# A two-layer post-norm decoder: the last step of the second attention, and who writes the two parts of the experts' down weights

## The chip, the cores and the metric

The program runs on one core of a Trainium2 chip. The metric is the time of one execution in microseconds (us), and the figure given for a kernel is the median of its runs. A core has TensorE (matrix products and transposes, PE in the profile; PEld is its weight load), VectorE (DVE), ScalarE (ACT), GpSimd (POOL) and SyncE (SP, which here only starts transfers). Each engine works through its own list of instructions in order; semaphores order them against each other. Matrix products and transposes write PSUM, eight banks of 512 float32 words per partition; the other working memory is SBUF.

## The reference

x has shape (4, 256, 256): four batches of 256 rows. Six sublayers follow one another, each in the form x = layernorm(x + f(x)):

```
x = LN(x + attention0(x));  x = LN(x + quantised cross product(x, fside, ctx));  x = LN(x + ternary FFN(x))
x = LN(x + attention1(x))          # stage 3 below: 16 heads, window 64, 4 sinks, output projection Wo
x = LN(x + cross attention(x, ctx))# stage 4: x @ softmax(q k^T), one 256x256 product per batch
x = LN(x + experts(x))             # stage 5: 8 experts, top 2, inner size 176
# experts:
probs = softmax(x @ gate_w.T);  combine = the two largest, divided by their sum
g, u = split(x @ w1[e].T);  out += combine[e] * (silu(g) * u) @ w2[e].T
```

All arithmetic is float32.

## The kernel before, in words

**Numbering.** A sublayer is a stage: 3 is the second attention, 4 the cross attention, 5 the experts. P is 128, S and D 256, B 4 batches; a pair is two batches. `x` holds the rows; `transpose_x(stage, lo, hi)` (L1856) turns the rows of some batches on TensorE into PSUM, and ScalarE's `evac_xT` (recorded at L813, the line of its helper `copy`) copies them to `xT`, from which the products of that stage read.

**Two parts.** The experts' products run in a float32 format that keeps fewer bits of an operand (fp32r), so each operand is split into a high part, the value rounded by writing it to that format, and a low part, the value less the high part. The up weights (`mw1H`, `mw1L`), the down weights (`mw2H`, `mw2L`) and x (`xH`, `xL`) have both. `up(n)` (L2424) makes 12 matmuls for one of 22 tiles of 512 columns, `down(n)` (L2441) 12 more.

**Weight groups.** Weights are loaded by DMA and turned by TensorE in groups of up to four 128x128 transposes into one bank (`pe_groups`, L397); the list is `G`, and `PLAN` has for each group its bank, the engine that copies it out, that engine's count, and the group that used the bank last. Groups 19 to 30 (NGM to NG2) are the 12 of the up weights, of 4, 4, 3, 4, 4, 3, ... transposes, 44 in all, in banks 0 and 1 in turn. VectorE writes their high part by a copy and their low part by a subtraction from PSUM (`evac_parts`, L1468 and L1469). They are turned beside the second attention: `beside(L, step, g)` gives the groups of each quarter step. Groups 31 to 36 (NG2 on) are the six of the down weights, 4 transposes each and 2 in the last, in banks 3 and 2 in turn. ScalarE copies each twice, to the high part and in full to `mw2f` (memory of `PT`); GpSimd subtracts the one from the other (L792). GpSimd also writes x's low part of the first pair for the experts (L787, semaphore `x_low0`).

**The second attention** (`attn_back(1)`) has six steps, 0 to 5, of four quarters g, each for four heads. In step s the scores' maxima of batch s are found and the exponentials, values and outputs of batch s-2 made; steps 4 and 5 so have only the latter. A quarter of TensorE in steps 4 and 5 is: `exp_scores(n)`, `values(n-1)` (L2084, L2087), the weight groups of `beside`, in g=1 `transpose_outputs` of the batch before (L2118), in g=2 its `project_outputs` (L2125), and `output_rows(n-1)` (L2094). VectorE in a quarter: `evac_parts` of the groups, in g=2 `attention_residual` (L1196), `divide_outputs` (L1411, L1415), and `norm_stats(3, 0)` in g=2 of step 4, `norm_apply(3, 0)` in g=0 of step 5. ScalarE: three exponentials (L957) and copies.

**After the last quarter** TensorE has this order: `transpose_x(4, 0, 2)`, once all up groups are copied out; `values(15)`; `context(0)`, the cross attention's product of batch 0 (L1869); `output_rows(15)`; `context(1)`; `transpose_outputs(3)`; `project_outputs(3)`; the six down groups; `transpose_x(5, 0, 2)`; `up(0)`; `logits(0)` (L2392); `up(1)`; `transpose_x(4, 2, 4)`; `context(2)`; `combine(0)` (L2400), which turns the experts' weights that VectorE's `router(0)` (L1729 to L1750) has made; `context(3)`; and then the loop `up(n)`, `down(n-2)` for n from 2 to 21. `up(1)` waits until all down groups are copied out, since it writes their banks, and `up(2)` for VectorE's `gated(0)` (L1765), which reads what `combine(0)` gave.

VectorE: `context_residual(0)`, `divide_outputs(15)`, `context_residual(1)`, `norm_stats(4, 0)` and `norm_apply(4, 0)` (L1207, L1216, L1223; between the two GpSimd makes the inverse deviations, L693 and L694), `attention_residual(3)`, `norm_stats(3, 2)`, `norm_apply(3, 2)`, `router(0)`, `copy_combine(0)`, `gated(0)`.

Of the kernel before, what the change touches and what calls it, by code (L numbers as in the profile page):

```python
# [5 lines left out]
def post_ln_decoder_two_layers(nc: bass.Bass, t: dict, out: bass.AP):  # L6
# [37 lines left out]
    with ExitStack() as ctx:  # L44
# [178 lines left out]
        mw2f = words_of(PT_words, 0, [P, EC, D])  # L223
# [84 lines left out]
        x_low0 = sem("x_low_part_of_pair0")  # L308
        mw2_low = sem("mw2_low_part")
# [43 lines left out]
        for c0 in range(0, EC, 2):  # L353
            n = min(2, EC - c0)
            group([m2n[:, r, c::EC] for c in range(c0, c0 + n) for r in range(2)],
                  [m[:, c0:c0 + n, :].rearrange("p a b -> p (a b)") for m in (mw2H, mw2L, mw2f)], P, n * 256, False, "m2")
# [11 lines left out]
        for k in range(len(G)):  # L368
            bank_ = k % 2 if k in BESIDE else 2 + k % 2 if k >= NG2 else k % 4
            eng_ = "act" if k >= NG2 or k in SHARED else "dve" if k in BESIDE or k % 2 else "act"  # L370
# [29 lines left out]
        def evac_groups(eng, copy, lo, hi, name):  # L400
            for k in range(lo, hi):
                srcs, dst, rows, cols, half, need = G[k]
                if PLAN[k][1] == name:
                    eng.wait_ge(wt_done, k + 1)
                    src = (bank16 if half else bank)(PLAN[k][0], cols, 0, rows)
                    if need == "m2":

                        copy(dst[0], src)
                        dst = dst[2]
                    copy(dst, src).then_inc(wt_act if name == "act" else wt_dve, 1)  # L410
# [25 lines left out]
        def xT_bank(stage, b):  # L436
# [3 lines left out]
            return b if stage == 4 and b < 2 else 6 + b % 2  # L440
# [13 lines left out]
        def beside(L, step, g):  # L454
# [5 lines left out]
            return lo + (hi - lo) * slot // (LAG * NG), lo + (hi - lo) * (slot + 1) // (LAG * NG)  # L460
# [191 lines left out]
        def _(pool):  # L652
# [131 lines left out]
            for b in range(2):  # L784
                bs = slice(b * S, (b + 1) * S)
                pool.wait_ge(xT_ready, turned(5, b))
                alone(pool.tensor_tensor(xL[5][:, :, bs], xT[:, :, bs], xH[5][:, :, bs].bitcast(F32), ALU.subtract),  # L787
                      x_low0)
            for k in range(NG2, len(G)):
                pool.wait_ge(wt_act, PLAN[k][2])  # L790
                high, low, full = G[k][1]
                alone(pool.tensor_tensor(low, full, high.bitcast(F32), ALU.subtract), mw2_low)  # L792
# [10 lines left out]
        def _(act):  # L803
# [156 lines left out]
            def attn_back(L):  # L960
                a = A[L]
                for step in range(STEPS):
                    for g in range(NG):
# [15 lines left out]
                        if g == 1 and step > LAG:  # L979
                            copy_OT(L, step - LAG - 1)  # L980
                if L == 1:
                    evac_xT(4, 0, 2)
                copy_outputs(L, B * NG - 1)
# [150 lines left out]
            evac_groups(act, copy, NG2, len(G), "act")  # L1134
            evac_xT(5, 0, 2)

# [31 lines left out]
        def _(dve):  # L1168
# [292 lines left out]

            def evac_parts(lo, hi):
# [19 lines left out]
            def attn_back(L):  # L1482
# [34 lines left out]
                if L == 1:  # L1517
                    context_residual(0)
                if L == 0:

                    copied_out(dve, NGM)
                    weight_maxima(0)
# [1004 lines left out]
```

## Time and profile before

| what | us |
|---|---|
| median of 3 runs | 480.86 |
| the runs | 477.39, 480.86, 483.25 |
| the profiled execution | 483.25 |
| its span, first to last instruction | 481.2 |
| outside the span | 2.05 |
| granted TensorE clock over the span, share of full speed | 0.932 |

A profile is one execution, recorded by the hardware. The busy time of an engine is the time in which it had an instruction under way; what stands in square brackets after an instruction is the idle time of its engine before it, and what ended it. A matmul's end is modelled, so starts are the better marks. All times below are us from the start of the span.

### The profile page before, as it was taken

The page shows a single profiled execution, that of the slowest core. Times are in us where ns is not written, and L with a number is a line of the kernel's source. Part 1 is how long each engine was busy: PE and PEld are TensorE (multiplying, and loading weights), DVE is VectorE, ACT ScalarE, POOL GpSimd, SP SyncE. Part 2 cuts the span into 40 slices and gives each one's busy share as a digit, 9 for nine tenths or more (in the row PEclk, how much of TensorE's full clock was granted, in tenths as well). Part 3 has the DMA queues.
Part 4 walks back from the last instruction along what each step waited for, and adds up shares of the span by engine and source line. Part 5 has one row for each costly group of instructions (what it writes and reads, how often), then busy time and mean ns, then how long its engine had stood idle before and what let it go on. Part 6 is the DMA issues. An engine that isn't in the chain of part 4 may idle for free.

```text
span 481.2 us, 8198 instructions
## 1 busy us (share of the span) xinstructions
PE 415.0 (86%) x3126; PEld 316.6 (66%) x3128; DVE 330.6 (69%) x768; ACT 245.5 (51%) x458; POOL 113.9 (24%) x134
## 2 busy tenths in 40 slices
PE   3976877999787776999997889999986999999993
PEld 2534644677655555789565755667665789888883
DVE  2499897777779888556567695458734685756555
ACT  1296903656646967566588434555516333523221
POOL 5500005538622451151563000001005310001001
PEclk9989797999999666699999899999988999999998
DMA  6900020000000000000000049810000000000101
GB/s 192 306 33 1 2 74 3 2 3 3 2 1 1 0 2 0 1 0 2 1 1 1 1 61 111 147 55 1 0 1 0 1 1 1 1 0 2 44 1 44
DMA packets 13126, 13.33 MB, mean 28 GB/s; under 512 B 2904, under 2 KB 12448, under 8 KB 12832
## 3 DMA queue, kind: packets, MB, share of 16 engines
q1 hardware_dynamic: 12224, 12.54, 11.5%
q8 instruction: 25, 0.41, 0.3%
q10 hardware_dynamic: 864, 0.27, 0.2%
q14 instruction: 13, 0.11, 0.1%
HBM read 11.56 MB, written 1.05 MB: 26 GB/s over the span
## 4 chain that ended last, share of the span: by engine, by line
PE 64%; DVE 20%; ACT 8%; DMA 3%; issue 3%; POOL 1%; SPq 0%; ACTq 0%; DVEq 0%; POOLq 0%
PE PS L2424 12%; PE PS L2441 6%; PE PS L1979 4%; ACT arena L813 4%; PE PS L2348 4%; PE PS L2084 4%; DVE mx L1400 3%; PE PS L397 3%; PE PS L2125 3%; PE PS L2364 3%; PE PS L2001 3%; PE PS L2052 3%; DMA arena<-mT 2%; DVE mx L1395 2%; PE PS L2094 2%
## 5 line engine op out<-in xcount | busy, mean ns | idle before, releaser
L957 ACT ACTIVATE PT<-PS 128x512 f32<-128x512 f32 x96 | 53.5, 595 | 35.9 <-PE PS L2052 35.8
L2424 PE MATMUL PS<-arena_r 128*128 128x512 f32 x264 | 66.0, 399 | 2.2 <-ACT xT L813 2.2
L2424 PEld LDWEIGHTS PS<-arena_r 128*128 128x128 f32 x264 | 49.2, 193 | 12.2 <-issue 2.6
L693 POOL TENSOR_SCALAR va<-mv 128x4 f32<-128x4 f32 x11 | 5.2, 475 | 195.9 <-DVE mv L1216 195.9
L813 ACT ACTIVATE arena<-PS 96x1024 bf16<-96x1024 bf16 (+6 forms) x59 | 42.2, 767 | 15.7 <-PE PS L1979 6.1
L1395 DVE TENSOR_REDUCE mx<-PS 128x4 f32<-128x512 f32 x32 | 21.9, 685 | 22.9 <-PE PS L2020 22.9
L2001 PE MATMUL PS<-masks,ident 128*128 128x512 bf16 x80 | 30.8, 386 | 5.8 <-DVE mx L1400 2.7
L2441 PEld LDWEIGHTS PS<-arena_r 128*128 128x128 f32 x264 | 34.4, 191 | 1.8 <-DVE arena_r L1773 0.2
L1400 DVE TENSOR_REDUCE mx<-PS 128x4 f32<-128x1024 f32 (+1 forms) x32 | 35.0, 1092 | 0.6 <-PE PS L2035 0.6
L1979 PE MATMUL PS<-ident,arena 128*96 128x128 bf16 x416 | 28.1, 229 | 8.1 <-ACT arena L813 4.7
L2441 PE MATMUL PS<-arena_r 128*128 128x256 f32 x264 | 35.0, 283 | 0.0
L1765 DVE TENSOR_TENSOR V<-PS,xb 128x512 f32<-128x512 f32 x22 | 15.2, 689 | 27.9 <-PE PS L2424 27.7
L1979 PEld LDWEIGHTS PS<-ident,arena 128*96 128x96 bf16 x416 | 26.1, 130 | 12.0 <-POOL arena L765 4.2
L1155 ACT ACTIVATE V<-PS 128x512 f32<-128x512 f32 x22 | 13.2, 600 | 37.1 <-PE PS L2424 37.1
L712 POOL TENSOR_SCALAR_AFFINE_SELECT PT<-PT 128x512 f32<-128x512 f32 x16 | 11.9, 741 | 70.3 <-ACT PT L957 70.0
L813 ACT ACTIVATE arena_r<-V 128x512 fp32r<-128x512 f32 x22 | 13.9, 632 | 24.9 <-DVE V L1769 24.9
L2084 PE MATMUL PS<-PT,V 128*32 128x256 f32 x256 | 21.1, 401 | 4.4 <-ACT PT L957 3.9
L1294 DVE COPY arena<-PS 96x1024 bf16<-96x1024 bf16 x32 | 21.0, 680 | 5.5 <-PE PS L1979 5.4
L2052 PE MATMUL PS<-arena 99*128 99x256 bf16 x128 | 22.7, 280 | 0.5 <-DMA arena<-mT 0.5
L2032 PE MATMUL PS<-arena 96*128 96x256 bf16 (+1 forms) x128 | 22.6, 264 | 0.4 <-DVE mx L1400 0.4
L397 PE MATMUL PS<-ident,arena 128*128 128x128 f32 (+2 forms) x150 | 21.0, 279 | 1.6 <-ACT PT L813 1.6
L813 ACT ACTIVATE OS<-PS 128x256 f32<-128x256 f32 x32 | 12.3, 384 | 18.4 <-PE PS L2087 18.4
(247 smaller groups left out, 949.8 us busy)
## 6 DMA issues: line engine op xcount, KB each, us to landing
arena<-in_L_ffn_w SPq DMA_DIRECT2D x16, 176.0 KB, 10.4
arena<-in_L_ffn_w SPq DMA_DIRECT2D x2, 1024.0 KB, 10.3
arena<-in_L_ffn_w SPq DMA_DIRECT2D x2, 704.0 KB, 6.7
arena<-in_fside_BxS2xS SPq DMA_DIRECT2D x1, 1024.0 KB, 12.2
out<-x SPq DMA_DIRECT2D x4, 256.0 KB, 2.2
x<-in_x SPq DMA_DIRECT2D x1, 768.0 KB, 9.1
arena<-in_L_attn_Wq SPq DMA_DIRECT2D x2, 256.0 KB, 4.5
arena<-in_L_attn_Wo SPq DMA_DIRECT2D x2, 256.0 KB, 6.1
```

Source lines behind the costliest of these rows:

```text
L397: last = nc.tensor.transpose(o, s, (ident16 if half else ident)[0:K, 0:K])
L813: return nc.scalar.activation(dst, src, ACT.Copy)
L957: nc.scalar.activation(PT[:, n % 2, 512 * j:512 * (j + 1)], bank(3 + j), ACT.Exp, scale=NEG_SCALE)\
L1395: v.tensor_reduce(mx[:, b % 2, 0, HG * g:HG * g + HG], bank(set_).rearrange("p (h s) -> p h s", h=HG), X, ALU.max).then_inc(a["mx"], 1)
L1400: v.tensor_reduce(mx[:, b % 2, 1, HG * g:HG * g + HG], PS[:, set_ + 1:set_ + 3, :].rearrange("p a (h s) -> p (a h) s", h=2) [:, :, 0:late_ ...
L1979: last = nc.tensor.transpose(bank16(4 + n % 4, P, i * P, STK), s_, ident16[:, :])
L2001: mm(out_, ident16[:, :], mk[:, cols].unsqueeze(1).to_broadcast([P, n_heads, cols.stop - cols.start]), start=start, stop=not start)
L2032: mm(bank(bk, keys.stop - keys.start, i * S), Qh[0:STK, b, h, P:S], K_[0:STK, b, kv(h), keys], start=(i == 0), stop=False)
L2052: last = mm(bank(bk, S, i * S), K_[0:R, b, kv(h), 0:P], Qh[0:R, b, h, :], start=(causal and i == 0), stop=(i == 1))
L2084: mm(PS[VW * i:VW * (i + 1), ob, 0:S], V1[:, 2 * b, kv(HG * g + i), :], p0[:, i, :], start=True, stop=False)
L2424: last = mm(bank(2 * (n % 2) + gu), wp[c][:, gu, c_ * P:(c_ + 1) * P], xp[5][:, c, blk * 512:(blk + 1) * 512], start=(step == 0 and c == 0 ...
L2441: last = mm(bank(4 + 2 * blk + k // 2, D, (k % 2) * D), amP[:, n % 3, part, k * P:(k + 1) * P], wp[:, c_, :], start=(c_ == 0 and k % 2 == ...
```

## The change

- **Down weights.** ScalarE makes one copy of each down group, the high part, and raises `m2_high`; VectorE writes the low part from PSUM (`m2_low`) and frees the bank. `mw2f`, the second copy and GpSimd's six subtractions go. TensorE turns the six groups two at a time in three places.
- **x's low part** of the first pair for the experts is made by VectorE (`low_x(5, 0, 2)`) and no longer by GpSimd.
- **Up groups.** `beside` deals the 12 out to six quarters, two each, so that the last two quarters have none.
- **Stage 4's turn and products.** `transpose_x(4, 0, 2)` moves into quarter g=2 of the last step, `context(0)` and `context(1)` into g=3.
- **Banks.** `transpose_x(5, 0, 2)` writes banks 4 and 5 and not 6 and 7, once the last exponentials have read them.
- **Order.** On TensorE `logits(0)` goes ahead of `up(0)` and `combine(0)` ahead of `context(2)`. On VectorE both context residuals and `norm_stats(4, 0)` go ahead of `divide_outputs(15)`; the low parts, `norm_stats(3, 2)` and `low_x(5, 0, 2)` stand among the rest as the diff shows.

```diff
@@ PLAN, evac_groups
-            eng_ = "act" if k >= NG2 or k in SHARED else "dve" if k in BESIDE or k % 2 else "act"
+            eng_ = "act" if k in SHARED else "dve" if k >= NG2 else "dve" if k in BESIDE or k % 2 else "act"
...
-                        copy(dst[0], src)
-                        dst = dst[2]
-                    copy(dst, src).then_inc(wt_act if name == "act" else wt_dve, 1)
+                        copy(dst[0], src).then_inc(m2_high, 1)
+                    else:
+                        copy(dst, src).then_inc(wt_act if name == "act" else wt_dve, 1)
@@ xT_bank, beside
-            return b if stage == 4 and b < 2 else 6 + b % 2
+            if b < 2 and stage >= 4:
+                return b if stage == 4 else 4 + b
+            return 6 + b % 2
...
-            return lo + (hi - lo) * slot // (LAG * NG), lo + (hi - lo) * (slot + 1) // (LAG * NG)
+            slots = LAG * NG if L == 0 else LAG * NG - 2
+            return min(hi, lo + (hi - lo) * slot // slots), min(hi, lo + (hi - lo) * (slot + 1) // slots)
@@ gpsimd
-            for b in range(2):
-                bs = slice(b * S, (b + 1) * S)
-                pool.wait_ge(xT_ready, turned(5, b))
-                alone(pool.tensor_tensor(xL[5][:, :, bs], xT[:, :, bs], xH[5][:, :, bs].bitcast(F32), ALU.subtract),
-                      x_low0)
-            for k in range(NG2, len(G)):
-                pool.wait_ge(wt_act, PLAN[k][2])
-                high, low, full = G[k][1]
-                alone(pool.tensor_tensor(low, full, high.bitcast(F32), ALU.subtract), mw2_low)
@@ scalar, attn_back
+                        if L == 1 and step == STEPS - 1 and g == 2:
+                            evac_xT(4, 0, 2)
+                copy_outputs(L, B * NG - 1)
                 if L == 1:
-                    evac_xT(4, 0, 2)
-                copy_outputs(L, B * NG - 1)
+                    evac_groups(act, copy, NG2, NG2 + 2, "act")
                 copy_OT(L, B - 1)
@@ scalar, after attn_back(1)
-            evac_groups(act, copy, NG2, len(G), "act")
+            evac_groups(act, copy, NG2 + 2, NG2 + 4, "act")
             evac_xT(5, 0, 2)
+            evac_groups(act, copy, NG2 + 4, len(G), "act")
@@ vector
+            def m2_low(lo, hi):
+
+                for k in range(NG2 + lo, NG2 + hi):
+                    _, (high, low), rows, cols, _, _ = G[k]
+                    dve.wait_ge(m2_high, k - NG2 + 1)
+                    v.tensor_tensor(low, bank(PLAN[k][0], cols, 0, rows), high.bitcast(F32), ALU.subtract).then_inc(wt_dve, 1)
@@ vector, attn_back
                 if L == 1:
                     context_residual(0)
+                    context_residual(1)
...
+                if L == 1:
+                    norm_stats(4, 0)
                 divide_outputs(L, B * NG - 1)
                 if L == 1:
-
-                    context_residual(1)
-                    norm_pair(4, 0)
+                    m2_low(0, 2)
+                    norm_apply(4, 0)
...
                 attention_residual(L, B - 1)
+                if L == 1:
+                    m2_low(2, 4)
@@ vector, after attn_back(1)
-            norm_pair(3, 2)
+            norm_stats(3, 2)
+            low_x(5, 0, 2)
+            m2_low(4, len(G) - NG2)
+            norm_apply(3, 2)
             router(0)
@@ tensor, transpose_x
                     elif stage == 4:
-                        pe.wait_ge(xT_ready, turned(5, b - 2))
+                        pe.wait_ge(out_read, 16)
                     elif stage == 5 and b < 2:
-                        pe.wait_ge(out_read, 16)
+                        pe.wait_ge(A[1]["pT"], 3 * B * NG)
@@ tensor, attn_back
+                        if L == 1 and step == STEPS - 1 and g == 3:
+                            pe.wait_ge(Xs["attT"], B)
+                            context(0)
                         if n >= 1:
                             values(n - 1)
+                        if L == 1 and step == STEPS - 1 and g == 2:
+                            transpose_x(4, 0, 2)
+                        if L == 1 and step == STEPS - 1 and g == 3:
+                            context(1)
...
-                if L == 1:
-                    transpose_x(4, 0, 2)
-                    pe.wait_ge(Xs["attT"], B)
                 values(B * NG - 1)
-                if L == 1:
-                    context(0)
                 output_rows(B * NG - 1)
                 if L == 1:
-                    context(1)
+                    pe.wait_ge(a["on"], B * NG - 1)
+                    pe_groups(pe, NG2, NG2 + 2)
                 transpose_outputs(B - 1)
@@ tensor, after attn_back(1)
-            pe_groups(pe, NG2, len(G))
+            pe_groups(pe, NG2 + 2, NG2 + 4)
             transpose_x(5, 0, 2)
+            pe_groups(pe, NG2 + 4, len(G))
+            logits(0)
             up(0)
-            logits(0)
             up(1)
             transpose_x(4, 2, 4)
+            combine(0)
             context(2)
-            combine(0)
             context(3)
```

## Rows read from the trace of the kernel before

**Rows 1.** The page's first part: busy time, share of the span and instructions of each engine.

```profile
PE 415.0 (86%) x3126; PEld 316.6 (66%) x3128; DVE 330.6 (69%) x768; ACT 245.5 (51%) x458; POOL 113.9 (24%) x134
```

**Rows 2.** The chain that ended last: start, length, engine, what it wrote, line.

```profile
349.79 1.06 PE PS L1856 x8
...
352.04 3.16 PE PS L1869 x8
355.42 1.73 PE PS L1869 x8
358.27 1.99 PE PS L2125 x8
368.51 4.42 PE PS L2424 x12
...
388.26 2.75 PE PS L2424 x12
```

**Rows 3.** Stretches: from:to and length, busy times and counts, granted clock, DMA.

```profile
339.64:383.83 44.19, 36.46 (x232) 28.61 (x229) 23.19 (x70) 17.83 (x35) 12.31 (x12) 0.92 0.00 1
...
350.85:355.30 4.45, 4.45 (x28) 3.21 (x28) 0.06 (x1) 1.07 (x3) 0.00 (x0) 0.62 0.00 0
368.50:372.90 4.40, 4.39 (x14) 3.52 (x15) 0.00 (x0) 0.00 (x0) 4.16 (x4) 0.65 0.00 0
383.83:472.30 88.47, 88.44 (x522) 78.41 (x521) 57.05 (x118) 30.66 (x49) 2.51 (x4) 1.00 0.02 7
321.00:339.64 18.64, 18.64 (x194) 13.64 (x193) 15.27 (x39) 10.98 (x24) 1.27 (x2) 1.00 0.01 4
```

**Rows 4.** Who TensorE waited for from 339 to 384: total us, times, longest.

```profile
PE PS L2424 <- ACT xT L813: 2.2, 1, 2.2
PE PS L1856 <- DVE arena_r L1469: 2.1, 1, 2.1
PE PS L397 <- ACT PT L813: 1.6, 4, 0.8
PE PS L1869 <- ACT xT L813: 0.9, 1, 0.9
PE PS L2125 <- ACT OT L813: 0.7, 1, 0.7
PE PS L2400 <- DVE xb L1750: 0.3, 1, 0.3
```

**Rows 5.** Groups by form, 320 to 348: count, busy us, mean ns, idle before.

```profile
L397 PE MATMUL PS<-ident,arena 128*128 128x128 f32 x44 | 6.6, 283 | 0.0
L1469 DVE TENSOR_TENSOR arena_r<-PS,arena_r 128x512 fp32r<-128x512 f32 x8 | 5.5, 691 | 0.3
L1468 DVE CAST arena_r<-PS 128x512 fp32r<-128x512 f32 x8 | 5.5, 689 | 5.9 <-PE PS L397 5.8
...
L1469 DVE TENSOR_TENSOR arena_r<-PS,arena_r 128x384 fp32r<-128x384 f32 x3 | 1.7, 557 | 0.1
```

**Rows 6.** The timeline, 363 to 382: start, length, instruction, idle time before.

```profile
363.04 1.40 DVE L1207 BATCH_NORM_STATS2 stat<-res 128x6 f32<-128x256 f32 x4
...
366.39 1.38 DVE L1223 TENSOR_SCALAR x<-res,mv,rstd 128x256 f32<-128x256 f32 x4 [1.55 <-POOL rstd L694]
...
367.69 0.67 ACT L813 ACTIVATE xT<-PS 128x512 f32<-128x512 f32 x1
...
370.34 7.54 POOL L792 TENSOR_TENSOR arena_r<-PT,arena_r 128x512 fp32r<-128x512 f32 x6
...
374.65 0.19 DVE L1729 TENSOR_REDUCE g<-PS 128x4 f32<-128x32 f32 x1 [6.88 <-PE PS L2392]
...
375.80 1.31 DVE L1734 TENSOR_TENSOR gp<-gp,g 128x32 f32<-128x32 f32 x1
...
381.06 0.43 DVE L1750 COPY xb<-gq 128x512 f32<-128x512 f32 x1
```

**Rows 7.** The timeline of VectorE, 413 to 420: the second router's same instruction.

```profile
414.51 0.19 DVE L1734 TENSOR_TENSOR gp<-gp,g 128x32 f32<-128x32 f32 x1
```

More of the change, by code:

```diff
@@ L222, in post_ln_decoder_two_layers @@
         mw2L = carve_parts(19200, [P, EC, D])
-        mw2f = words_of(PT_words, 0, [P, EC, D])
         fT = carve(19456, [P, B, DC, S])
@@ L307, in post_ln_decoder_two_layers @@
         x_low = sem("x_low_part")
-        x_low0 = sem("x_low_part_of_pair0")
-        mw2_low = sem("mw2_low_part")
+        m2_high = sem("mw2_high_part")
         G = []
@@ L355, in post_ln_decoder_two_layers @@
             group([m2n[:, r, c::EC] for c in range(c0, c0 + n) for r in range(2)],
-                  [m[:, c0:c0 + n, :].rearrange("p a b -> p (a b)") for m in (mw2H, mw2L, mw2f)], P, n * 256, False, "m2")
+                  [m[:, c0:c0 + n, :].rearrange("p a b -> p (a b)") for m in (mw2H, mw2L)], P, n * 256, False, "m2")
         LOADS = {"l0": 16 * 3, "wo0": 16, "f": 16, "c": 16, "w1": 16, "w2": 16, "l1": 16 * 5, "xw": 32, "gate": 16,
@@ L402, in evac_groups @@
                 srcs, dst, rows, cols, half, need = G[k]
-                if PLAN[k][1] == name:
+                if (PLAN[k][1] if need != "m2" else "act") == name:
                     eng.wait_ge(wt_done, k + 1)
@@ L2418, in up @@
                     if step == 1 and c_ == 0:
-                        pe.wait_ge(x_low if blk else x_low0, B + 2 if blk else 2)
+                        pe.wait_ge(x_low, B + 2 * blk + 2)
                     for gu in range(2):
@@ L2434, in down @@
                     copied_out(pe, len(G))
-                    pe.wait_ge(mw2_low, len(G) - NG2)
                 if c_ == 0:
```

## The prediction

> **What bounds the kernel now.** Read the busy times first [rows 1]: TensorE is busy for 86% of the span, VectorE for 69%, GpSimd for 24%. That suggests TensorE but doesn't say where it waits. The chain that ended last [rows 2] tells more: around the change it is almost TensorE alone, and two of its steps are too long. A `context` product takes 3.16 us at 352.04 and 1.73 at 355.42; an `up` takes 4.42 us at 368.51 and 2.75 later. [...] The excess is 3.16 - 1.73 = 1.4 and 4.42 - 2.75 = 1.7, in all 3.1 us.
>
> The same rows bound the change. Behind 383.83, where `up(2)` starts, TensorE is busy for 88.44 of 88.47 us at full clock. Nothing the change does can shorten that, and the end moves by as much as the start of `up(2)` does. Ahead of 339.64, the start of the second attention's last but one quarter, TensorE is busy without a break from 321 on. So what can be won lies in the 44.19 us between: 36.46 busy, 7.73 idle. The waits [rows 4] add up to that: 2.2 for x's turn before `up(0)`; 2.1 for the last up group's low part; 1.6 in four pieces for the down groups, whose bank waits for ScalarE's second copy; 0.9 for x's turn before `context(2)`; 0.7 for the attention outputs' copy; 0.3 for the router. Idle and excess are 10.8 us, the ceiling of any gain here. Useful work is 44.2 - 10.8 = 33.4 us.
>
> **Part by part.**
>
> **Up groups earlier.** Eleven of the 44 transposes leave the last two quarters for earlier ones. At 6.6 / 44 = 0.15 us busy each, overlapped [rows 5], that is at most 1.6 us, by starts about 1.25; TensorE pays there what it saves here: 0. The transposes of x in g=2 find x ready if VectorE has copied all groups out. VectorE was busy 15.27 of 18.64 us from 321 to 339.64 [rows 3]; now come three more groups, two of 0.69 + 0.69 and one of 0.55 + 0.56 [rows 5], 3.9 us, so 19.2 us of work in 18.64 + 1.25 = 19.9. That just fits, but g=0 of the last step also has a `norm_apply` of 1.38 [rows 6]. Laying the quarters out by these durations, I get two short waits of TensorE for VectorE, 0.45 in g=0 and 0.75 before x's transposes. They take the place of the 2.1 us wait. The ends: 0, if the slack suffices, and 2.1 as before, plus the 1.4 us of lower clock. I take 1.2, by the load.
>
> **Context products in g=3.** `context(0)` and `context(1)` now run between products that are ready. They are the same work at 1.73 to 1.9 us each, but x's copies, which ScalarE makes under `project_outputs(2)`, don't lie before them, and there is no lower clock if the long wait before them is gone: 1.4 us saved. What remains is the copy of the outputs of head group 15 before `output_rows(15)`: it was hidden by `context(0)` and now is not. The nearest row is the 0.7 of the same kind of wait at L2125 [rows 4]; the copy is half as wide, so 0.55.
>
> **VectorE's order before the last division.** Behind `context(1)` VectorE has 2 x 0.69 for the residuals (as an operation of 128x512 from PSUM, [rows 5]), then the statistics: from their start at 363.04 to `norm_apply` at 366.39, less 1.55 idle, 1.8 us [rows 6]. Only then comes `divide_outputs(15)`, 0.5. TensorE meanwhile has `output_rows(15)` and two down groups, about 1.0 us. By my layout the statistics end at 357.5, the division at 358.0, and TensorE waits from 356.3 to 358.1: 1.8 us of new wait. `transpose_outputs(3)`, the copy's 0.7 (kept) and `project_outputs(3)` end at 361.3; it was 360.3. This part alone so is 1 us later, with two down groups (1.0) already done inside it.
>
> **Down groups and x's parts.** ScalarE's six second copies (0.6 each) go; the four waits of 1.6 go with them. The bank now comes free by ScalarE's copy and then VectorE's subtraction, 0.69 from PSUM [rows 5], but between groups of one bank stands other work: `transpose_outputs` and `project_outputs` for the first pair, x's transposes for the second. I leave 0.15 for the last group. The wait of 2.2 us before `up(0)` was the four copies of x behind two copies of down groups. Now the two last transposes and groups (0.8) run beside the copies: I get 0.85, ends 0.5 and 2.2. `project_outputs` at 361.3, two groups to 362.2, x's turn to 363.3, groups to 364.2, copies ready at 365.05, `logits(0)` to 366.8, `up(0)` to 369.6, `up(1)` to 372.5, x's turn to 373.5. At full clock that saves the 1.7 us of excess.
>
> **The router in front.** This is what will be late next. Behind `attention_residual(3)`, at 361.5 at the earliest, VectorE has in one row: 0.7; two low parts 1.4; statistics 1.8; two of x's low parts 1.4; two more low parts 1.1 (the last group is half as wide); `norm_apply` 1.4; the router. GpSimd no longer takes the low parts at 7.54 / 6 = 1.26 us each, VectorE does at 0.69. The subtractions are 3.9 us of this row that weren't in it. The router ran from 374.65 to 381.49, 6.84 us. One of its instructions took 1.31 us while GpSimd was subtracting [rows 6] and 0.19 in the second router, with GpSimd idle [rows 7]; another was stretched by about 0.36. GpSimd has nothing there now: 6.84 - 1.12 - 0.36 = 5.4 us. With small gaps the row ends at 375.1, 1.6 us behind TensorE, which therefore waits 1.6 us before `combine(0)`. Before, `context(2)` stood there and hid it. Then 0.66 for `combine`, 2 x 1.9 for the contexts (x's copies are ready: the wait of 0.9 goes, and the 0.3): `up(2)` starts at 379.6.
>
> [...]
>
> **The sum.** New waits: 0.45 + 0.75 + 0.55 + 1.8 + 0.7 + 0.15 + 0.85 + 1.6 = 6.85. Old waits and excess: 7.7 + 3.1 = 10.8. The gain is 4.0; by the layout from start to start (383.83 - 379.6) 4.2. Behind `up(2)` nothing changes: the down parts are wanted earlier but ready earlier. I say 4.2 us. The profiled execution took 483.25, so 479.05 for its like, with a span of 477.0; the median of the runs lies 2.4 below it, so 480.86 - 4.2 = 476.7. Two per cent is 9.6 us, about what a measurement of this kernel can tell from no change, so this falls within it.
>
> **The rivals.**
> (a) *The clock falls in the new waits.* It fell behind waits of 2.1 and 2.2 us and behind none of 0.9 or less. The new ones of 1.8 and 1.6 lie between. Each spell costs 1.4 to 1.7. The one behind 358 would be paid in full; one in `up(0)` would be hidden by the router's row; one behind `combine(0)` would be paid. So 1.7 us with one (478.4), 3.4 with two (480.1). The other side of the line is one more: if VectorE's backlog in the last step makes the wait before x's transposes 2.1 us or more and the clock falls there too, a third spell and 1.4 us more wait give 4.2 - 3.4 - 1.4 - 1.4 = -2.0, slower: 482.9. It decides from the point at which three waits reach that length. For it speaks VectorE's load of 19.2 in 19.9; against it, that two waits are under 1 us by the layout. [...]
> (b) *VectorE's row is longer than I have it*: the router as slow as before, and a handover between engines before each low part. 1.5 + 1 us: gain 1.7, 479.2.
> (c) *VectorE keeps up*: no wait for the up groups, the division early, the router's row hidden. 1.2 + 1.0 + 1.6 more: gain 8.0, 472.9.
> (d) *It doesn't do what it says*: the two big waits stay under other names (the last up group before x's transposes, x's copies before `logits(0)`), each with its lower clock. Then only the 1.6 and 0.9 go and the router's 1.6 comes: gain 1, 479.9.
>
> **How the numbers follow.** Forecast, gain 3 to 5.5: 0.45. (a) with one or two spells 0.17, with three 0.04. (b) 0.13. (c) 0.10. (d) 0.08. Something else 0.03. Predicted 476.7. The range must take in (c)'s nearer half and all of (a) with two spells, (b) and (d); the runs before lie 3.5 below and 2.4 above their median, so a median of a few has some 2 us of its own: 472 to 481.5. Faster by more than 9.6 us would need nearly the whole ceiling of 10.8 or a low draw: 0.05. Slower by more than 9.6 has no mechanism here: 0.02. Within: 0.93.
>
> **What would show it.** Right, if the profile after has: x's transposes for stage 4 in the last but one quarter with a wait under 1 us; both `context` at 1.9 us; a wait of 1.5 to 2 us for VectorE before the last L2118; no wait of 2 us before `logits(0)`; a wait for L1750 before `combine(0)`; the router's L1734 at 0.19; TensorE unbroken from `up(2)`, at 379 to 380; GpSimd's L787 and L792 gone, about 10 us of busy time. The forecast is wrong if the granted clock falls in more than one place from 345 on, or if the wait before `combine(0)` is over 3 us.

## The result, and the profile after

| | before | changed |
|---|---|---|
| median, us (12 runs each) | 480.85 | 474.81 |
| lowest to highest | 477.39 to 483.25 | 472.49 to 479.0 |
| profiled execution, span | 483.25, 481.2 | 475.2, 473.5 |

The ratio is 0.9886, 95% interval 0.9855 to 0.9917: 5.5 us faster, 4.0 to 7.0. The forecast was 476.7, a gain of 4.2. The prediction held that a change under two per cent could hardly be told from none; this one is 1.1% and clear of the noise.

The two spans differ by 7.7 us, and not all of that is the change. Take two marks: the second attention's first `project_outputs` (312.64 before, 309.56 after) and the start of `up(2)` (383.83 [rows 3] and 376.02). The first profile after was 3.1 us ahead before any of the moved or new instructions ran; from `up(2)` to the end it takes 97.5 us against 97.4. **The stretch between the marks is what the change touches: 71.19 us before, 66.46 after, 4.7 us less.** A second profile of the changed kernel gives 66.43 with the first mark at 311.64. A run also takes 0.35 us less outside the span (475.2 - 473.5 = 1.7 against 2.05); no run says why. The stretch is the main measure below, but it comes from one profile of each kernel, so the ratio of whole runs, which scatter by several us but are 4 to 12, is read beside it. Two profiles are of the slowest run of their kernel, the one before (483.25) and that of turn_and_groups_back below (483.63 of 475.44 to 483.63), and their stretches stand for the long end.

The stretches as windows; columns: length, busy time and count of PE, PEld, DVE, ACT, POOL, then granted clock, DMA share and GB/s. Before:

```profile
312.64:383.83 71.19, 63.46 (x504) 47.97 (x503) 43.09 (x119) 32.43 (x65) 13.58 (x14) 0.95 0.03 11
```

After:

```profile
309.56:376.02 66.46, 62.57 (x503) 48.07 (x503) 47.68 (x130) 30.66 (x61) 4.36 (x6) 0.95 0.04 11
```

TensorE's idle time falls from 71.19 - 63.46 = 7.7 to 3.9 us, GpSimd's work from 13.6 to 4.4, VectorE's rises by 4.6. The mean clock is as low as before. The chain that ended last, after (answers to [rows 2]):

```profile
340.23 1.06 PE PS L1865 x8
...
344.56 1.78 PE PS L1878 x8
347.13 1.92 PE PS L1878 x8
...
354.59 3.59 PE PS L2134 x8
...
363.74 7.20 PE PS L2436 x24
371.56 0.98 ACT xT L805 x2
372.68 3.69 PE PS L1878 x16
376.38 2.77 PE PS L2436 x12
```

Both first `context` products now take under 2 us (L1878); but `project_outputs(3)` (L2134) takes 3.59 where it took 1.99 before [rows 2], and the first two `up` (L2436) 7.20 where 2 x 2.75 [rows 2] is usual. Who TensorE waited for, 335 to 384, after (answers to [rows 4]):

```profile
PE PS L2127 <- DVE on L1410: 1.3, 1, 1.3
PE PS L2134 <- ACT OT L805: 0.7, 1, 0.7
PE PS L2404 <- ACT xT L805: 0.5, 1, 0.5
PE PS L2103 <- ACT OS L805: 0.5, 1, 0.5
PE PS L1878 <- ACT xT L805: 0.4, 1, 0.4
PE PS L1865 <- DVE arena_r L1471: 0.3, 1, 0.3
```

Neither wait of 2 us is left. In front of `transpose_outputs(3)` (L2127) stands the new one for VectorE's division. Two stretches of the profile after show why two steps are slow all the same: the clock was granted at 0.54 and 0.50. By slices of 1 us it reads 0.50 from 355 to 357 and from 365 to 368, and 1.00 from 353 to 354, 358 to 359, 363 to 364 and 369 to 370.

```profile
356.00:358.00 2.00, 2.00 (x6) 1.57 (x5) 0.00 (x0) 0.00 (x0) 0.00 (x0) 0.54 0.00 0
...
366.00:368.00 2.00, 2.00 (x7) 1.51 (x6) 1.47 (x8) 1.51 (x2) 0.00 (x0) 0.50 0.00 0
```

The router, after: no stretched instruction, none of the 128x32 ones over 0.20 us, and it ends 0.6 us before TensorE wants it at L2412.

```profile
366.88 0.19 DVE L1740 TENSOR_TENSOR gp<-gp,g 128x32 f32<-128x32 f32 x1
...
370.66 0.43 DVE L1756 COPY xb<-gq 128x512 f32<-128x512 f32 x1
...
371.64 0.60 PE L2412 MATMUL PS<-ident,xb 128*128 128x128 f32 x4
```

### The profile page after: what moved, and what is told of

The parts are those of the page before. It is cut to its first block, busy times and chain, and to the rows that moved or that the text cites. A ratio compares the mean times of both kernels' runs of the same rounds, so it can differ in the third digit from the quotient of the medians.

```text
span 473.5 us, 8188 instructions
## 1 busy us (share of the span) xinstructions
PE 409.9 (87%) x3128; PEld 314.2 (66%) x3128; DVE 334.3 (71%) x776; ACT 243.2 (51%) x452; POOL 105.3 (22%) x126
## 4 chain that ended last, share of the span: by engine, by line
PE 60%; DVE 24%; ACT 8%; DMA 3%; issue 3%; POOL 1%; SPq 0%; ACTq 0%; DVEq 0%; POOLq 0%
PE PS L2436 13%; PE PS L2452 7%; ACT arena L805 4%; PE PS L2360 4%; DVE mx L1395 3%; PE PS L1988 3%; PE PS L2134 3%; PE PS L2376 3%; PE PS L2093 3%; PE PS L395 2%; DMA arena<-mT 2%; PE PS L2010 2%; PE PS L2061 2%; DVE mx L1390 2%; PE PS L2103 2%
## 5 line engine op out<-in xcount | busy, mean ns | idle before, releaser
L2436 PE MATMUL PS<-arena_r 128*128 128x512 f32 x264 | 66.0, 400 | 0.0
L2436 PEld LDWEIGHTS PS<-arena_r 128*128 128x128 f32 x264 | 49.4, 193 | 9.7
L713 POOL TENSOR_SCALAR_AFFINE_SELECT PT<-PT 128x512 f32<-128x512 f32 x16 | 11.9, 743 | 66.2 <-ACT PT L949 65.9
L2360 PE MATMUL PS<-arena_r 128*128 128x512 f32 x64 | 20.7, 448 | 0.6 <-ACT arena L805 0.5
```

The source lines that it names most:

```text
L2360: last = mm(bank(n % 2), w1T[:, c, f * P:(f + 1) * P], part[:, c, blk * 512:(blk + 1) * 512], start=(i == 0 and c == 0), stop=(i == 1 and ...
L2436: last = mm(bank(2 * (n % 2) + gu), wp[c][:, gu, c_ * P:(c_ + 1) * P], xp[5][:, c, blk * 512:(blk + 1) * 512], start=(step == 0 and c == 0 ...
```

## The experiments

Theory 1 was the prediction's: the gain is TensorE's waits that went and the lower clock behind them. Theory 2: it comes from taking the low parts off GpSimd. The third question was the clock. All stretches run from the first `project_outputs` to `up(2)`, one profile each; the last column is the ratio of whole runs to runs of the kernel before on the same chip. The kernels ran on three chips, so ratios compare better than medians; filled, filled_logits and the three division kernels have four runs each, the others ten. A spell is a stretch in which the clock was granted at 0.50; behind the same waits, within 0.01 us, `project_outputs(3)` took 3.59 us in the changed kernel's profile and 2.00 in that of logits_back, so a difference of about 1.6 us between two stretches can be the clock alone.

| kernel | stretch, us | median | ratio (95%) |
|---|---|---|---|
| before | 71.19 | | |
| changed | 66.46, again 66.43 | 475.89 (again) | 0.9884 (0.9850 to 0.9918) |
| turn_and_groups_back | 73.00 | 479.96 | 0.9965 (0.9920 to 1.0010) |
| turn_in_tail | 66.56 | 477.87 | 0.9930 (0.9895 to 0.9965) |
| low_on_gpsimd | 69.32 | 478.01 | 0.9971 (0.9931 to 1.0012) |
| low_after_norm | 66.77 | 477.04 | 0.9926 (0.9888 to 0.9964) |
| filled | 64.87 | 474.48 | 0.9882 (0.9825 to 0.9939) |
| filled_logits | 64.62 | 473.67 | 0.9852 (0.9784 to 0.9921) |
| logits_back | 64.61 | 476.11 | 0.9910 (0.9869 to 0.9951) |
| before_filled | 68.35 | 480.07 | 0.9986 (0.9950 to 1.0021) |
| division_first | 63.49 | 472.89 | 0.9833 (0.9771 to 0.9895) |
| division_order | 62.95 | 472.99 | 0.9852 (0.9789 to 0.9915) |
| division_order_filled | 62.98 | 472.74 | 0.9835 (0.9766 to 0.9905) |

**1. The changed kernel again.**

> The changed kernel once more, beside the others. Stretch from the first project_outputs of the second attention to up(2): 66.5 us in its first profile against 71.2 before. Theory 1: it repeats within 1 us, up to the 1.7 us of a spell of lower clock more or less, whatever the time of the whole run; the 3.1 us by which the first profile was ahead when it came to the second attention have nothing to do with the change and come out differently. If they do come from the change, the second profile again reaches that product at 309.6 and not at 312 or so.

The stretch repeats within 0.03 us, slow steps included (`project_outputs(3)` 3.56; the two `up` 7.34, 7.33 by the same view of the first profile). The first mark came at 311.64, not 309.6: 2.1 of the 3.1 us of lead ahead of it are scatter. Over the 14 profiles of this study it lies between 307.96 and 312.64. The two profiles of the kernel before, with and without fillers, are the latest (312.09 and 312.64), so that a part of the lead belongs to the change is neither shown nor excluded.

**2. x's turn, the context products and the up groups back.**

```diff
-            slots = LAG * NG if L == 0 else LAG * NG - 2
+            slots = LAG * NG
...
-                        if L == 1 and step == STEPS - 1 and g == 2:
-                            transpose_x(4, 0, 2)
-                        if L == 1 and step == STEPS - 1 and g == 3:
-                            context(1)          # context(0) and evac_xT(4, 0, 2) likewise
...
+                    transpose_x(4, 0, 2)        # behind the last quarter, as before the change
...
```

> The changed kernel with the up groups dealt to eight quarters again and x's turn for stage 4 and both context products again behind the last quarter; the down weights, x's low part and the order on TensorE stay changed. Theory 1 (the gain is the waits that went): the 2.1 us wait for the last up group's low part and the lower clock behind it come back, 0.3 + 0.5 us of small waits go; 2.5 to 3.5 us slower than the changed kernel, so 477 to 478.5, ratio to before about 0.994. Theory 2 (the gain comes from the low parts leaving GpSimd): as fast as the changed kernel, 474 to 475.5.

In this profile the stretch is 6.5 us longer than the changed kernel's, twice what was expected, and 1.8 longer than before. Whole runs say less: a median of 479.96 against 475.89 and 474.81, and 0.9965 (0.9920 to 1.0010), so not slower than the kernel before. Its TensorE timeline; in brackets the idle time before:

```profile
348.62 1.38 PE L1865 MATMUL PS<-ident,x 128*128 128x128 f32 x8 [2.11 <-DVE arena_r L1471]
...
351.37 2.61 PE L1878 MATMUL PS<-attT,xT 128*128 128x256 f32 x8
...
358.85 0.66 PE L2127 MATMUL PS<-ident,on 128*128 128x128 f32 x4 [1.96 <-DVE on L1410]
360.19 3.78 PE L2134 MATMUL PS<-woT,OT 128*128 128x256 f32 x8 [0.69 <-ACT OT L805]
...
368.63 2.63 PE L2403 MATMUL PS<-gwT,xT 128*128 128x8 f32 x16 [0.97 <-ACT xT L805]
371.12 8.25 PE L2435 MATMUL PS<-arena_r 128*128 128x512 f32 x24
```

The wait of 2.11 is back to the hundredth, and there are three spells: at the first context behind it (2.61), at `project_outputs(3)` (3.78) and at the two `up` (8.25), with the clock granted at 0.50 from 350 to 352, 360 to 366 and 371 to 376. The wait for the division is 1.96 and not 1.26. In this profile it is what the prediction's rival (a) describes with three spells.

**3. Only the turn and the products back**, the groups dealt early (the same diff without its first two lines).

> The changed kernel with x's turn for stage 4 and both context products again behind the last quarter, the up groups dealt to six quarters as in the change. Theory 1: TensorE waits for x's copies no longer than before, since values(15) covers them, and the up groups are copied out in time; the division of the last outputs waits for the same statistics, which end at about the same time; 0 to 1 us slower than the changed kernel. If moving the context products is what counts, 2 us or more slower.

```profile
353.96 0.71 PE L2127 MATMUL PS<-ident,on 128*128 128x128 f32 x4 [1.96 <-DVE on L1410]
355.36 3.78 PE L2134 MATMUL PS<-woT,OT 128*128 128x256 f32 x8 [0.69 <-ACT OT L805]
...
365.51 5.74 PE L2435 MATMUL PS<-arena_r 128*128 128x512 f32 x24
```

66.56, 0.1 more than the changed kernel. Between this and experiment 2 stands only `beside`: VectorE's last copy is done in time when the groups are dealt early, and the wait of 2.11 is gone. In these two profiles that is 73.00 - 66.56 = 6.4 us of stretch, but waits make up only 1.6 of it (6.2 and 4.6 us in all) and the rest is the clock; by whole runs it is about 2 us (479.96 and 477.87), with intervals that overlap. The products' place isn't settled. The stretch says that moving them is worth 0.1 us, although the wait for the division is 0.7 longer here. Whole runs say about 2 us: 0.9930 against 0.9886 and 0.9884, with intervals that overlap.

**4. The low parts back on GpSimd.**

```diff
+                        copy(dst[2], src).then_inc(wt_act, 1)     # the full copy again
...
             inverse_deviations(4, 0)
+            m2_lows(0, 4)                                        # GpSimd
             inverse_deviations(3, 2)
+            # x's low part of batches 0 and 1, then m2_lows(4, 6); none of the three on VectorE
```

> The changed kernel with ScalarE's second copies of the down groups back, and GpSimd again writing the down weights' low parts and x's low part of the first pair. Theory 1 (TensorE arrives last at combine(0), as in the profile after, 371.64 against 371.09 for the router): the 3.9 us of subtractions leave VectorE's row, the router starts earlier but is stretched beside GpSimd, up(2) starts within 0.7 us of where it did; same time as the changed kernel. Theory 2 (the low parts' place is the gain): 3 to 4 us slower, 478 to 479.

Theory 1 expected no change, and it was wrong: 2.9 us more in the stretch, and by whole runs 0.9971 against 0.9886 and 0.9884, about 4 us. VectorE, then GpSimd (L790 down weights, L799 x), then what TensorE waited for:

```profile
352.69 3.44 DVE L1235 TENSOR_SCALAR x<-xb,mv,rstd 128x256 f32<-128x256 f32 x4 [1.12 <-POOL rstd L699]
...
352.73 2.60 POOL L790 TENSOR_TENSOR arena_r<-PT,arena_r 128x512 fp32r<-128x512 f32 x2
...
363.19 5.02 DVE L1235 TENSOR_SCALAR x<-res,mv,rstd 128x256 f32<-128x256 f32 x4 [3.76 <-POOL rstd L699]
...
363.23 2.64 POOL L799 TENSOR_TENSOR arena_r<-xT,arena_r 128x512 fp32r<-128x512 f32 x2
...
373.52 0.66 PE L2424 MATMUL PS<-ident,xb 128*128 128x128 f32 x4 [2.79 <-DVE xb L1770]
```

`norm_apply` is four instructions of 0.41 us, 1.38 in all [rows 6]. Beside GpSimd's subtractions it took 3.44 and 5.02. The deviations it waits for also came late (3.76 us idle), since they stand on GpSimd behind four subtractions: the last two ran from 359.10 for 2.63 us, the deviations' L698 and L699 from 361.81. The router, behind both, ended 2.8 us after TensorE was there. The wait for x's copies before the logits is also longer, 1.38 us against 0.55.

**5. GpSimd's subtractions moved off `norm_apply`**, x's low part on VectorE as in the change.

```diff
             inverse_deviations(3, 2)
+            pool.wait_ge(x_normed, normed(3, 3))
+            m2_lows(0, len(G) - NG2)
```

> The kernel with the low parts on GpSimd, changed so that the down weights' low parts start behind norm_apply(3, 2) and x's stay on VectorE. In low_on_gpsimd the two norm_apply took 3.44 and 5.02 us where they take 1.38 alone, each beside GpSimd's subtractions of 1.3. Theory of contention: both are back at 1.4 us, the wait for the router of 2.8 us goes, stretch 66 to 67 as in the changed kernel. If GpSimd's work as such were the cause (its queue, the second copies on ScalarE), the stretch stays at 69 or so.

```profile
354.68 1.99 PE L2141 MATMUL PS<-woT,OT 128*128 128x256 f32 x8 [0.69 <-ACT OT L816]
...
L1229 DVE TENSOR_SCALAR x<-res,mv,rstd x4: 403/404/405, 361.9 to 362.8; 128x256 f32<-128x256 f32 x4
```

The second line gives minimum, median and maximum in ns: `norm_apply` is back at 0.40 us apiece, and the stretch at 66.77. The contention moved to the router: three instructions that take 0.19 alone took 1.10 (L1752), 0.93 (L1755) and 1.33:

```profile
368.93 1.33 DVE L1753 TENSOR_TENSOR gr<-gr,order 128x32 f32<-128x32 f32 x1
```

Others took 0.95 and 0.55; the router's reductions stayed at 0.19 beside the same subtractions. Although it began at 363.25, it ended at 372.62, and TensorE waited 1.38 us for it. The stretch is only 0.3 us above the changed kernel's, but by luck of the clock: `project_outputs(3)` took 1.99 here, at a granted 1.00, and 3.59 there. An estimate with equal clocks is 0.3 + 1.6 = 1.9 us, and whole runs agree (0.9926 against 0.9886 and 0.9884, about 2 us). So the low parts on GpSimd, with ScalarE's second copies, cost about 2 us where they keep clear of `norm_apply`, and about 4 by whole runs where they meet it. What share the late deviations had was not separated.

**6. Matmuls that nobody reads in the waits.**

```diff
                 values(B * NG - 1)
+                if L == 1:
+                    idle_products(4, 2)          # 512 columns, bank 4, free by then
                 output_rows(B * NG - 1)
...
                     pe_groups(pe, NG2, NG2 + 2)
+                    idle_products(4, 5)
                 transpose_outputs(B - 1)
+                if L == 1:
+                    idle_products(4, 3)
...
             pe_groups(pe, NG2 + 4, len(G))
+            idle_products(6, 2)
             logits(0)
```

> The changed kernel with twelve matmuls of 512 columns that nobody reads in four of TensorE's waits: 2 before output_rows(15), 5 after the first two down groups, 3 between transpose_outputs(3) and project_outputs(3), 2 before logits(0). Theory 1 with the clock: the waits stay as long, the clock doesn't fall, project_outputs(3) takes 1.9 us and not 3.6 and the first two up tiles 5.6 and not 7.3; the router's row then ends last and takes back part: 2 to 3 us faster than the changed kernel, 472 to 473. Without an effect of the waits on the clock: the same, or slower by up to 1 us where a filler is longer than its wait.

`project_outputs(3)` took 1.99 us instead of 3.59, the stretch is 1.6 shorter. Whole runs, four of them, show no gain over the changed kernel (474.48, 0.9882), where 2 to 3 us were expected. The two `up` stayed slow, without any wait before them:

```profile
359.67 0.59 PE L1896 MATMUL PS<-masks,ident 128*128 128x512 bf16 x2
360.38 2.13 PE L2409 MATMUL PS<-gwT,xT 128*128 128x8 f32 x16
362.37 7.18 PE L2441 MATMUL PS<-arena_r 128*128 128x512 f32 x24
```

```profile
360.00:362.00 2.00, 1.88 (x17) 1.62 (x15) 1.97 (x8) 1.10 (x3) 0.82 (x2) 1.00 0.00 0
362.00:364.00 2.00, 2.00 (x7) 1.71 (x8) 2.00 (x6) 0.00 (x0) 1.00 (x1) 0.50 0.00 0
```

TensorE is busy for 1.88 of the first 2 us, at a granted clock of 1.00, and for all of the second, at 0.50. What came just before the fall are the 16 matmuls of 8 columns of `logits(0)`.

**7. The same with `logits(0)` behind `up(0)`**, as before the change.

> The filled kernel with logits(0) behind up(0) again. In the filled kernel the clock fell at 362 without any wait, behind 0.6 us of transposes, two matmuls and 16 matmuls of 8 columns. If those 16 let it fall, the first two up tiles now run at full clock, 5.6 us and not 7.2, and TensorE then waits for the router, whose logits come 2.8 us later but which VectorE reaches only then: stretch 64.9 less 0 to 1. If the clock falls for another reason, up(0) is slow again and the stretch is 64.9 to 65.5.

```profile
360.66 3.01 PE L2441 MATMUL PS<-arena_r 128*128 128x512 f32 x12 [0.21 <-ACT xT L805]
363.51 1.85 PE L2409 MATMUL PS<-gwT,xT 128*128 128x8 f32 x16
365.21 2.98 PE L2441 MATMUL PS<-arena_r 128*128 128x512 f32 x12
...
370.80 0.66 PE L2417 MATMUL PS<-ident,xb 128*128 128x128 f32 x4 [1.73 <-DVE xb L1756]
```

Both `up` are at full clock (granted 1.00), 3.0 each. TensorE then comes early and waits 1.73 us for the router: nearly all is given back, 64.62 against 64.87. The prediction's wait of 1.6 us before `combine(0)` is here.

**8. `logits(0)` behind `up(0)` in the changed kernel, without fillers.**

> The changed kernel with logits(0) behind up(0), as before the change, nothing else and no fillers. If the 16 matmuls of 8 columns let the clock fall, project_outputs(3) is still slow (3.6 us) but both up tiles run at 2.8 to 3.0; TensorE is then 1.8 us early at combine(0) and waits for the router there: stretch 66.0 to 66.8, no gain. If the order of logits matters for the router, the stretch is 1 us or more longer.

```profile
353.90 2.00 PE L2134 MATMUL PS<-woT,OT 128*128 128x256 f32 x8 [0.69 <-ACT OT L805]
...
359.60 3.00 PE L2436 MATMUL PS<-arena_r 128*128 128x512 f32 x12 [0.64 <-ACT xT L805]
```

64.61, better than expected, because `project_outputs(3)` ran at full clock too (granted 1.00, 2.00 us), behind waits of 0.50, 1.25 and 0.69 us; behind 0.51, 1.26 and 0.69 it took 3.59 in the changed kernel. With those 1.6 us back it would be 66.2, as expected, and whole runs show no gain either: 476.11 and 0.9910 against 0.9886 and 0.9884. So whether that step is slow is not decided by those waits alone. Of the six profiles with these waits and no filler (the changed kernel twice, turn_in_tail, where the middle one is 1.96, low_on_gpsimd, low_after_norm and this one), it was slow in four, 3.56 to 3.78.

**9. Fillers in the kernel before.**

> The kernel before the change with matmuls of 512 columns that nobody reads in its three longest waits: 8 ahead of x's turn for stage 4, 3 between transpose_outputs(3) and project_outputs(3), 8 ahead of up(0). It tells how much of the change's gain is the clock alone. By the excess of its rows (1.4 and 1.7 us) the stretch goes from 71.2 to about 68, the whole 3 us faster than before, ratio 0.994. If the waits have nothing to do with the clock it stays at 71.2 or more.

```profile
351.03 1.99 PE L1869 MATMUL PS<-attT,xT 128*128 128x256 f32 x8
...
366.33 3.02 PE L2427 MATMUL PS<-arena_r 128*128 128x512 f32 x12 [0.45 <-ACT xT L813]
```

The stretch is 68.35, 2.8 us less, with `context(0)` at 1.99 instead of 3.23 and `up(0)` at 3.02 instead of 4.42, both at a granted 1.00; expected was 68. Whole runs don't show it: 0.9986, interval 0.9950 to 1.0021, where 2.8 us would be 0.9942. So the 2.8 is the price of two spells, not a gain to count on. How often the kernel before has both stays open. An estimate says not always: its shortest run on record is 474.99, and less 2.05 outside the span, 97.4 behind `up(2)` and 307.96, the earliest first mark of any profile, that leaves 67.6 us for the stretch, if its first mark came no earlier.

**10. The division first.**

```diff
+                divide_outputs(L, B * NG - 1)
                 if L == 1:
                     norm_stats(4, 0)
-                divide_outputs(L, B * NG - 1)
-                if L == 1:
                     m2_low(0, 2)
```

> The changed kernel with divide_outputs(15) ahead of norm_stats(4, 0) on VectorE, nothing else. Theory 1: the wait of 1.26 us before the last transpose_outputs goes, project_outputs(3) starts 1.2 us earlier and up(2) 1 to 1.3 us earlier, stretch 65.2 to 65.5; if the clock then stays up behind the remaining 0.7 us wait, up to 1.8 us more, 63.5. Rival: the statistics only come later and the inverse deviations with them, so x's turn for stage 5 waits for norm_apply(4, 0) and nothing is won.

```profile
351.23 0.60 PE L2126 MATMUL PS<-ident,on 128*128 128x128 f32 x4
352.57 1.99 PE L2133 MATMUL PS<-woT,OT 128*128 128x256 f32 x8 [0.74 <-ACT OT L805]
...
356.97 1.08 PE L395 MATMUL PS<-ident,arena 128*128 128x128 f32 x6 [0.57 <-DVE arena_r L1462]
```

The wait of 1.26 is gone, `project_outputs(3)` is at full clock (granted 1.00, 1.99 us), and the stretch is 63.49: 3.0 us less, as the more hopeful end had it. A wait of 0.57 for a low part is new. By waits the order that the change chose for VectorE was a mistake of 1.2 us: the wait of 1.26 and the 0.55 before the logits are gone, 0.57 is new. The other 1.8 us are busy time, most of it the spell that is missing; that it stays away because of the division isn't shown, since two profiles with the old order were without it too (experiments 5 and 8).

**11 and 12. Division first, with both orders on TensorE as before the change**, without and with fillers.

> division_first (stretch 63.5) with logits(0) behind up(0) and combine(0) behind context(2), both as before the change. Both up tiles at full clock would bring TensorE to combine(0) 1.8 us sooner; context(2) then covers the router, at the price of 0.9 us of waiting for x's copies: stretch 62 to 62.8, and 471 to 472.5 us for the whole. Rival: the clock falls elsewhere in the same place, stretch 63.5 or more.

> division_order with matmuls that nobody reads in the waits that are left: 2 ahead of output_rows(15), 3 ahead of project_outputs(3), 2 ahead of up(0). If the waits of 0.5 and 0.7 us alone let the clock fall now and then, this is steadier and up to 1.8 us faster than division_order; if they don't, it is the same within 0.3 us in the stretch.

Both `up` are at full clock (granted 1.00; 3.30 and 3.02 us, with fillers 3.33 and 3.03), `context(2)` covers the router, and it costs 0.89 us of waiting for x's copies as before: 62.95 and 62.98, just above the 62 to 62.8 expected. The fillers add nothing here. By whole runs the three last kernels can't be told apart (0.983 to 0.985); each is faster than the kernel before by 0.8% at the least, and their medians, 472.7 to 473.0, lie 2 to 3 us below the changed kernel's two, 474.8 and 475.9.

**The two theories.** Neither holds alone. By whole runs 1.1% is gained; with the groups and the turn back 0.35% is left (experiment 2), with the low parts back on GpSimd 0.29% (experiment 4). Each takes back most of the gain, so the parts depend on each other and their shares can't be added up.

## Why the prediction was right

**Where TensorE waits now.** The forecast of 4.2 us stands beside 4.7 in the stretch and 5.5 (4.0 to 7.0) in whole runs. The argument that the end moves by as much as `up(2)` held: 97.4 and 97.5 us behind it.

**The terms.** Idle time was oversized and the clock left out. That the two errors nearly cancel is luck:

| term | predicted | measured |
|---|---|---|
| waits for up groups | 0.45 + 0.75 | 0.30 |
| copy before `output_rows(15)` | 0.55 | 0.51 |
| the division | 1.8 | 1.26 |
| copy before `project_outputs(3)` | 0.7 | 0.69 |
| down group's bank | 0.15 | 0 |
| x's copies before the logits | 0.85 | 0.55 |
| router before `combine(0)` | 1.6 | 0; instead 0.45 for x's copies |
| lower clock | 0 | 1.60 + 1.70 |

Idle was put at 6.85 and is 3.8; the clock's excess was put at 0 and is 3.3 (3.59 - 1.99 and 7.20 - 5.50). Together 6.85 against 7.1. The rest of the 4.7 is busy time: with 3.3 us of excess in it, against 3.1 before, it still fell from 63.5 to 62.6. For 0.45 of that the rows give a cause: the down groups' 22 transposes took 3.80 us in five pieces with waits between them and take 3.35 in three rows. The rest isn't traced.

**Up groups earlier.** Right: with the groups back beside the turn, the 2.11 us wait returns to the hundredth; with the turn back and the groups still early it stays away (experiments 2 and 3). The groups alone were not put back. VectorE kept up better than the layout had it, 0.30 for 1.2.

**The statistics ahead of the division.** Right in mechanism, 1.26 for the 1.8 that the layout had; experiment 10 removes the wait. It is below the 1.5 to 2 us that the prediction named as its sign.

**The clock.** The excess of 1.4 and 1.7 us that the prediction counts in the kernel before lies where the granted clock is 0.62 and 0.65 [rows 3]; slices of 1 us read 0.50 from 352 to 354 and from 369 to 371, and 1.00 from 355 to 356 and from 372 to 383. This step failed, by the prediction's own sign: "The forecast is wrong if the granted clock falls in more than one place from 345 on". The sum put nothing for it, from the rows of before ("It fell behind waits of 2.1 and 2.2 us and behind none of 0.9 or less"), and one or two spells, rival (a), had 0.17. Both profiles of the changed kernel have two, worth 3.3 us. One came behind waits of 0.5, 1.3 and 0.7; the other behind `logits(0)`, whose move ahead of `up(0)` was costed at nothing. The number came right all the same, since one spell was hidden by the router's row and the waits before it were shorter than forecast. In eight profiles with the logits ahead the two `up` took 7.18 to 8.25 us in six, and 6.11 and 5.74 in two, whose granted clock there was 1.00; in the five with the logits behind and no wait over 0.7 us in front, each `up` took 2.98 to 3.33. So the order bears on the spell but doesn't decide it alone. The first spell came behind idle time; but the same waits, within 0.01 us, stood ahead of a granted 1.00 in experiments 5 and 8. The second, as experiment 6 shows it, came behind 2 us with TensorE busy for 1.88. What sets a spell off no run shows.

**The router in front.** The row was as long as forecast (5.4 us of router: 365.73 to 371.09) but began 0.9 us earlier against the first mark, and the slow `up` hid it: the wait for the router before `combine(0)`, named as a sign, is missing in both profiles. Where they are fast, the wait of 1.7 us is there (experiments 7 and 8). So the forecast wait of 1.6 and the spell of 1.7 in `up` stand for the same time, and the prediction's words that a spell there "would be hidden by the router's row" were right: taking it away won 0.25 us (64.87 to 64.62).

**GpSimd.** The prediction took 1.12 + 0.36 = 1.5 us off the router for the time it had beside GpSimd's subtractions, and nothing off `norm_apply`. Experiments 4 and 5 show more: where the subtractions meet `norm_apply`, 1.4 us become 3.4 and 5.0. In the kernel before they hardly met (`norm_apply` from 366.39 for 1.38 us, [rows 6]; GpSimd's parts of x from 367.53, its down groups from 370.34); in experiment 4's order they did. With the low parts on VectorE, as in the change, GpSimd makes none of these subtractions: both `norm_apply` took 1.38 us (354.31 and 364.44) and the router's L1740 0.19. The router's stretched instructions have two tensor inputs, `norm_apply` has one; and the same router line, L1753 in low_after_norm, took 0.19 us at 366.09 and 1.33 at 368.93, each 0.01 us behind the start of a subtraction. What decides whether an instruction is stretched no run shows.

**The rivals.** (c), VectorE keeps up, came true for most of the up groups' wait and a third of the division's. (d) is excluded by the waits. (b) didn't occur. (a) occurred with two spells, yet without its loss. Its three spells are in the one profile of turn_and_groups_back, with a stretch 1.8 us longer than before; that kernel's whole runs are not slower than before.

## What to carry to other kernels

Ask of a waiting step what it would cost to deal its last producer's work out earlier: here that removed a wait of 2.1 us, wherever the products stood. Put what another engine waits for ahead of what only its own later work needs, even for 1.8 us of statistics; and look at what runs on GpSimd during each VectorE `tensor_scalar` or `tensor_tensor`: beside GpSimd's subtractions 1.38 us became 3.44 and 5.02 and 0.19 became up to 1.33, and which ones met changed with the schedule. Measure such edits by a stretch between two marks of the trace when whole runs scatter by more than the gain, but compare the granted clock inside it before reading a difference: the same step behind the same waits took 3.59 us in one profile and 2.00 in another, and only whole runs average over that (the changed kernel's twelve have mean clocks of 0.938 to 0.963).

## What the runs showed of the hardware that was not expected

- The granted clock fell from 1.00 to 0.50 behind 2 us in which TensorE was busy for 1.88, the last of it 16 matmuls of 8 columns (2.13 us, filled). With the same products behind a full `up`, the next `up` took 2.98 us at a granted 1.00 (filled_logits).
- Behind the same waits (0.50 or 0.51, 1.25 or 1.26, 0.69 us) the granted clock was 1.00 in two profiles (1.99 and 2.00 us for `project_outputs(3)`, low_after_norm and logits_back) and fell to 0.50 in three (3.56, 3.59, 3.78; after_again, after, low_on_gpsimd).
- Four `tensor_scalar` instructions of 128x256, 1.38 us in all, took 3.44 and 5.02 us beside GpSimd subtractions of 128x512 (low_on_gpsimd); a 128x32 `tensor_tensor` of 0.19 us took up to 1.33, while 128x32 reductions beside the same subtractions stayed at 0.19 (low_after_norm).
- The point at which one kernel's profiles reach the second attention differed by 2.1 us (309.56 and 311.64) with nothing changed; the mean granted clock up to there was 0.92 and 0.91.
